# Zero blocks, cell scatters and gather waits rearranged in a graph attention and GCN kernel

## What is computed

```python
q, k, v = (typed_linear(x, W, ntype) for W in (Wq, Wk, Wv))
a  = (typed_rel(k[src], rel_att, etype) * q[dst]).sum(-1) * rel_pri / sqrt(D)
ex = exp(a - segment_max(a, dst)[dst])
h  = segment_sum(typed_rel(v[src], rel_msg, etype) * ex / segment_sum(ex, dst)[dst], dst)
x  = layernorm(x + layernorm(x + gate * typed_linear(h, Wa, ntype) + (1 - gate) * x))
for W, b, g, be in layers:          # three GCN layers, edge weights ew, self loops added
    norm = dinv[src] * ew * dinv[dst]
    h = batch_norm(segment_sum((h @ W)[src] * norm, dst) + b)   # relu between layers
out = layernorm(x + h)
```

## Time and profile before

| what | us |
|---|---|
| median of 3 runs (4591.87 to 4594.39) | 4593.5 |
| the profiled execution | 4592.2 |
| its span | 4590.3 |
| batches 2 to 51, by SP's issues | 1599.9 |
| last attention gather to L537 | 119.9 |
| L537's end to the first dense matmul | 373.2 |

### The profile page before, as it was taken

How to read it: one execution, slowest core, us unless ns; L and a number is a source line. 1 busy time by engine, 2 the same in 40 slices (tenths; PEclk the granted TensorE clock), 3 DMA queues, 4 the chain that set the end, 5 groups by cost and what they waited for, 6 DMA issues and landing times. The chain is left out here.

```text
span 4590.3 us, 52237 instructions
## 1 busy us (share of the span) xinstructions
PE 2969.0 (65%) x14449; PEld 2143.5 (47%) x14449; DVE 2312.5 (50%) x8186; ACT 1147.0 (25%) x2512; POOL 2411.3 (53%) x2514
## 2 busy tenths in 40 slices
PE   3895666666676666664420666777767776767774
PEld 3774656666666656663200433344433444433342
DVE  3774655655655555553522345533455534455435
ACT  1223556555655555552001200000000000000001
POOL 0002544444466666665577266665466664666662
PEclk9998778777787877776755889988899988999987
DMA  4896555565422322221000455555545545555552
GB/s 110 273 358 232 199 200 210 189 216 191 163 88 80 87 79 81 84 81 48 1 1 0 172 190 174 189 191 184 186 174 190 189 174 179 192 188 176 189 189 61
DMA packets 232026, 706.47 MB, mean 154 GB/s; under 512 B 62326, under 2 KB 111957, under 8 KB 212928
## 3 DMA queue, kind: packets, MB, share of 16 engines
q1 hardware_dynamic: 104252, 447.79, 26.7%
q0 software_dynamic: 93184, 191.21, 14.4%
q10 hardware_dynamic: 34308, 64.13, 4.3%
HBM read 559.66 MB, written 143.28 MB: 153 GB/s over the span
## 5 line engine op out<-in xcount | busy, mean ns | idle before, releaser
L552 POOL DMA_INDIRECT stage<-h_tab,earr x1248 | 1183.3, 948 | 810.8 <-issue 346.5
L527 POOL DMA_INDIRECT arena<-kv_tab,idxr x832 | 796.0, 957 | 970.3 <-ACT idxr L634 405.6
L1013 PE MATMUL bank<-arena,xr 128*128 128x512 f32 (+1 forms) x2058 | 1021.1, 638 | 5.6 <-issue 5.6
L992 PE MATMUL bank<-oh,stage 128*128 128x128 f32 x2496 | 394.3, 308 | 494.0 <-issue 487.8
L992 PEld LDWEIGHTS bank<-oh,stage 128*128 128x128 f32 x2496 | 354.1, 214 | 712.3 <-issue 701.1
L860 PE MATMUL bank<-xr,arena 128*128 x3328 | 494.0, 308 | 236.8 <-DVE arena L1254 146.9
L1572 DVE TENSOR_TENSOR sums<-sums,bank 128x128 f32 x1248 | 351.3, 282 | 568.3 <-remote 398.2
L1013 PEld LDWEIGHTS bank<-arena,xr 128*128 128x128 f32 x2058 | 407.6, 212 | 394.8 <-issue 394.8
L860 PEld LDWEIGHTS bank<-xr,arena 128*128 128x128 f32 x3328 | 456.0, 218 | 259.3 <-issue 258.2
L499 POOL DMA_INDIRECT a_tab<-tot,cell x416 | 416.0, 1000 | 261.2 <-DMA arena<-kv_tab,idxr 151.1
L709 ACT ACTIVATE rs<-mv,epsc 128x49 f32<-128x49 f32 (+1 forms) x6 | 1.9, 316 | 2003.3 <-DVE mv L1611 1692.6
(11 more groups left out here) (224 smaller groups left out, 2739.4 us busy)
## 6 DMA issues: line engine op xcount, KB each, us to landing
arena<-a_tab SPq DMA_DIRECT2D x147, 1792.0 KB
a_tab<-stage SPq DMA_DIRECT2D x49, 1792.0 KB
kv_tab<-stage SPq DMA_DIRECT2D x48, 768.0 KB, 8.5
arena<-key_d ACTq DMA_DIRECT2D x52, 512.0 KB, 7.1
arena<-ew_d ACTq DMA_DIRECT2D x52, 512.0 KB, 10.1
arena<-rel_d SPq DMA_DIRECT2D x52, 512.0 KB
stage<-h_tab,earr POOLq DMA_INDIRECT x1248
arena<-kv_tab,idxr POOLq DMA_INDIRECT x832
```

Of the source, the lines that this page charges most:

```text
L527: G.indirect_dma_start(kv[b % 3][:, t, :], None, kv_tab, bass.IndirectOffsetOnAxis(idxr[:, b % 3, t:t + 1], 0))\
L552: G.indirect_dma_start(gring[:, (q % NG) * GRP + s, :], None, h_tab[l], bass.IndirectOffsetOnAxis(src_i[:, t:t + 1], 0)).then_inc(row_land ...
L992: last = M.matmul(bank[q % NG][:, s * P:(s + 1) * P], gring[:, (q % NG) * GRP + s, :], oh[:, q % NG, s, :], start=True, stop=True)
L1013: mm = M.matmul(o_[:, 0:cw], xr[:, n, :], abuf[B % NBUF][:, n % KB, 0:cw], start=n == 0, stop=n == NT - 1)
```

## The change

Three things are done.

1. `zeros_by(b)` becomes `b * NBLK // ZB` with ZB = 46: one zero block for each of batches 1 to 46, two for b = 16, 31 and 46.
2. No scatter stands between gathers. SY = 120 scatters follow the last gather, 296 follow L537.
3. Ahead of every group but the first (batch edges included), POOL waits for three of the four gathers of the group before (`kv_land` at 48) and, through the new semaphores `kv_last`, for the fourth gather of the group before that. DVE and ACT wait for both, so for all four of the group that they use.

```diff
-SB = 28
-SPB = 6
-SY = 48
-ZPB = 2
+SY = 120
+ZB = 46
...
-    zeros_by = lambda b: min(NBLK, ZPB * b)
+    zeros_by = lambda b: min(NBLK, b * NBLK // ZB)
...
+        kv_last = [sem(f"kv_last{a}") for a in range(2)]
...
                 for g in range(NG):
-                    if g:
-                        pool.wait_ge(kv_land[b % 3][g - 1], 64 * (b // 3 + 1))
-                    for t in slots.get((b, g), ()):
-                        scatter(t)
+                    n = NG * b + g
+                    if n:
+                        b_, g_ = (n - 1) // NG, (n - 1) % NG
+                        pool.wait_ge(kv_land[b_ % 3][g_], 48 * (b_ // 3 + 1))
+                    if n >= 2:
+                        pool.wait_ge(kv_last[n % 2], 16 * (n // 2))
                     if b >= 3:
                         pool.wait_ge(vw_ready, NG * (b - 3) + g + 1)
...
-                         .then_inc(kv_land[b % 3][g], 16)
+                         .then_inc(kv_land[b % 3][g] if s < GRP - 1 else kv_last[n % 2], 16)
             for b in range(NB):
                 gather(b)
-            for t in range(first_of, first_of + SY):
+            pool.wait_ge(tot_ready, 1)
+            for j in range(ND):
+                pool.wait_ge(a_zeroed[j], 16 * BPC)
+            for t in range(SY):
                 scatter(t)
...
-            for t in range(first_of + SY, T1):
+            for t in range(SY, T1):
                 scatter(t)
...
-                dve.wait_ge(kv_land[b % 3][g], 64 * (b // 3 + 1))
+                dve.wait_ge(kv_land[b % 3][g], 48 * (b // 3 + 1))
+                dve.wait_ge(kv_last[g % 2], 16 * ((NG * b + g) // 2 + 1))
```

More of the change, by code:

```diff
@@ L98, in gnn @@
     assert NT % KB == 0 and 2 * T1 == ET and T1 <= 512 and 512 * (ND - 1) < WD and WA + TPB <= 512 * ND and GT % GRP == 0
-    assert HALF + WD <= NW and T1 % KT == 0 and zeros_by(SB - 3) == NBLK
+    assert HALF + WD <= NW and T1 % KT == 0 and ZB < NB
     def groups_before(d):
@@ L502, in _ @@
             pool.wait_ge(tabs_complete, 1)
-            slots, first_of = {}, 0
-            for b in range(SB, NB):
-                for k in range(SPB):
-                    slots.setdefault((b, k % NG), []).append(first_of)
-                    first_of += 1
             def gather(b):
@@ L512, in gather @@
                 pool.sem_inc(gathers_begun, 1)
-                if b == SB:
-                    pool.wait_ge(tot_ready, 1)
-                    for j in range(ND):
-                        pool.wait_ge(a_zeroed[j], 16 * BPC)
                 for g in range(NG):
-                    if g:
-                        pool.wait_ge(kv_land[b % 3][g - 1], 64 * (b // 3 + 1))
-                    for t in slots.get((b, g), ()):
-                        scatter(t)
+                    n = NG * b + g
[4 more added lines that the diff above has]
+                        pool.wait_ge(kv_last[n % 2], 16 * (n // 2))
                     if b >= 3:
@@ L632, in indices @@
                     for g in range(NG):
-                        act.wait_ge(kv_land[b % 3][g], 64 * (b // 3))
+                        act.wait_ge(kv_land[b % 3][g], 48 * (b // 3))
+                    for a in range(2):
+                        act.wait_ge(kv_last[a], 16 * (NG // 2) * (b - 2))
                 S.activation(idxr[:, b % 3, :], idx_c[:, bass.ds(b * TPB, TPB)], ACT.Copy).then_inc(idx_ready, 1)
```

## The result

The changed kernel takes 4644.1 us (median of 4 runs, 4632.4 to 4653.8) where the kernel before takes 4592.7 in the same measurement: a ratio of 1.0114, 95% interval 1.010 to 1.0129. It is slower by 1.1%; the forecast was 4557, faster. Its profiled execution takes 4632.4 us with a span of 4630.6, at the lower end of the four, 40.3 us above the span of before. In the changed code the gathers are L518, the scatters L498, the large add is L531 (before: L537), the negative and zero loads of SP are L431 and L438, the first GCN gather L546, the dense matmul L1009, the first matrix load L454.

A forecast was written before the change was run, and what follows sets the result against it. No engine is busy above 65%; POOL's waits for gathers bound free attention batches, scatter bursts slow the stretch behind. Terms -188 + 85 + 68 = -35 against 4592.2 gave 4557 us, range 4445 to 4650.

The forecast's parts named there:

- attention to the last gather: Attention batches: shorter by 188 us, from scatters out about -155, pauses about -130, zeros about +100.
- 72 more scatters ahead of the add: Last gather to L537: the longer burst adds 85 us, bounds +34 and +106.
- 72 more behind it: L537 to the first dense matmul: the longer burst adds 68 us, bounds +55 and +97.
- GCN layers after that: GCN layers behind the first dense matmul: untouched, each keeping its length.
- the free batch, 24.6 us: Attention batch without zeros or scatters: falls from 27.3 to 24.6 us by waiting for the third gather.
- The zero block, 4.7 us,: Attention: a single zero block adds 4.7 us to its batch, as much as a pair does.
- Rival (b): Attention: a single zero block costs half of a pair, 106 us less, total 4451 us; chance 0.11.
- the rule that the prediction cites: DMA queues: an engine alternates between queues with work, packet by packet, so a gather's delay follows from its own packets.
- the factor of 5.7 of the second burst: Scatters behind L537: a pair of tiles slows from 2.45 to 14.05 us; also applied ahead of L537.
- (a): Both scatter bursts: other work proceeds at less than a tenth, +106 and +118, total 4628 us; chance 0.20.
- The 1.47 us a scatter: Scatters behind L537: they complete every 1.47 us, slower than issued, which sets when the matrix loads start.
- (c): Attention: the third gather's landing gives nothing, free batches stay at 27.3 us, total 4689 us; chance 0.09 with its halves.

The follow-up runs named there:

- second chip: Another chip, where both kernels ran again unchanged: before 4340.7 us, the change 4322.7 us, ratio 0.9959.
- the looser waits: POOL waits for all four gathers of the group before last, not three of the last; on the kernel before 3926.5 us, on the change 3985.8 us.
- the change with pairs: The changed kernel with its zero blocks again in pairs, in batches 1 to 25: 4265.4 us, 0.9816 of the kernel before.
- the paced burst: The changed kernel with each scatter waiting until the one four before it has completed: 4319.1 us, 0.9938 of the kernel before.
- the pauses alone: The kernel before with only the change's new POOL waits, zero pairs and scatters left as they were: 4179.1 us, 0.9622.

## Why the prediction was wrong

In the terms of its sum, with the first measurement's profile and the experiments:

| term | forecast | measured first | second chip |
|---|---|---|---|
| attention to the last gather | -188 | -144 | -188 |
| 72 more scatters ahead of the add | +85 | +102 | +93 |
| 72 more behind it | +68 | +76 and +15 in the first layer | +93 |
| GCN layers after that | 0 | -8 | -2 |
| sum | -35 | +40 | -5 |

- **The first step that failed is the free batch, 24.6 us.** Of its four groups, two or three are as worked out: pauses of 1.3 to 1.5 us, periods of 6.0 to 6.5 us in the changed kernel against 7.28. The others, in which or behind which SP's loads are issued, take 6.6 to 8.4 us, and a free batch takes 26.4. On the second chip, where SP issues the loads from 1869.68 to 1871.5, that pause reads 3.31 us beside two of 1.32:

```profile
1864.02 0.95 POOL L518 DMA_INDIRECT arena<-kv_tab,idxr  x1 [1.32 <-DMA arena<-kv_tab,idxr]
...
1870.38 0.95 POOL L518 DMA_INDIRECT arena<-kv_tab,idxr  x1 [1.32 <-DMA arena<-kv_tab,idxr]
...
1878.39 0.95 POOL L518 DMA_INDIRECT arena<-kv_tab,idxr  x1 [3.31 <-DMA arena<-kv_tab,idxr]
```

  DVE's own chain, which I took as 24.0 us, is nearer 23.5: the 6.6 us of waiting fell in a window of 48 us and not in two whole batches, and with the looser waits batches take 23.4 (and 3 x 7.28 + 4 x 1.25 is 26.8, not 26.9). Over batches 7 to 46 the rate missed by 30.27 - 29.3 = 1.0 us, 39 us in all, over the last four by 1.8, 7 us. Two of SP's three loads there are small, 64 KB each, but the third (L426) moves 512 KB. In the 25 free batches of the change with pairs, the first of POOL's pauses that ends more than 3 us behind its issue is 2.9 us on average, the others 1.4. That this load is what holds up the landing is only argued: no run moved it.
- **The zero block, 4.7 us,** was right in kind (one costs what two cost, 3.8 to 4.2) and 0.8 too high, which takes back part of the first error. Rival (b) is refuted. Spreading the blocks cost some 60 us (the change against the change with pairs, on two chips), where I had "about +100" within the sum. The packets around the change's block of 1104.75 show what holds the group up. The group's four gathers are issued from 1104.11 to 1107.86 on the software queue (q0), the block goes on the hardware queue (q1). The DMA rows (packets, MB, share of the engines) of 1107 to 1111 us, and then of 1111 to 1115:

```profile
q1 hardware_dynamic: 395, 1.42, 100.0%
q0 software_dynamic: 3, 0.01, 1.3%
```

```profile
q1 hardware_dynamic: 200, 0.67, 47.0%
q0 software_dynamic: 144, 0.39, 26.4%
```

  For 4 us the block has the engines to itself and the gathers' own packets stand still; they don't take turns with it packet by packet, as in the rule that the prediction cites. With the pair of 1173.73 in the kernel before, none of the gathers' packets moves from 1176 to 1179 us, and then 143 move beside 447 of the block's queue until 1184: the second block runs beside them, which is why two cost hardly more than one.
- **The scatters ahead of the add, +85.** I took 19 us of the burst as work done under it, by the factor of 5.7 of the second burst. The rows show less: DVE's stalls grow with the burst, up to 42.82 us, and the add comes 221.8 us behind the last gather where (a) forecast 226; in the forecast's terms 106 - 102 = 4 us of the work were done under the burst and not 19. The failing step is the use of one burst's factor for the other. On the other chips the size is right for another reason: DVE isn't slowed, is done before POOL, and the 72 issues count in full.
- **Behind the add, +68.** The matrix load follows the add's end by 427 us (forecast 435) and the dense matmul by 449 (441): mis-sized by 8. But I called the GCN gathers harmless, and they start 15 us behind the dense matmul, where before they started 6 us ahead of it; the first layer takes 14.7 us more. That the late gathers are the reason isn't tested by itself, but the kernel with eight scatters a batch shows the same pair: gathers 20 us behind the dense matmul, a first layer 18 us longer. Together +91, close to the upper bound of +97. The 1.47 us a scatter behind it are refuted as a rate by the paced burst; what looked like a rate is a fixed 40 us on the last ones.
- **The chances.** The result is near rival (a) in its first half and between the forecast and (a) in the second; in the free batches it lies two thirds of the way from the forecast to (c) (26.4 between 24.6 and 27.3). That (a)'s sum of +36 meets the measured +40 is luck: its terms were -188, +106 and +118, where -144, +102, +91 and -8 were measured. (a) had 0.20; the forecast's sum of -35 stood on three terms of 68 to 188 us, which turned out to be off by 44, 17 and 23, so more of the chance belonged on the other side.
- **What the forecast didn't look at** is that the waits themselves make zeros and scatters expensive. "POOL idles until the fourth gather has landed" was read as the price of a free batch. It is also what turns one block into 4 us and six scatters into 6 to 8. With the looser waits one or two blocks cost nothing, and six scatters 28.2 - 23.4 = 4.8 us, where POOL's own issuing (27.7) has become the bound; that is no less than the 4.2 beside the new pauses, so the scatters' price didn't go away. Part 1 of the change touches the blocks, part 2 the scatters, and only the third, the waits, works on the cause, and on the kernel before it does better alone (0.9622) than with the other two (0.9959).

Adding up, on the chips of the experiments: pauses -164 us (before to the pauses alone), scatters moved behind the last gather +86, single blocks for pairs +57, together -21, beside the measured -18 to -21. The three are steps of one path from before to the change, so that their sum must agree is no test; what it gives is the price of each part in this order. The second of them by its parts: 144 scatters cost 144 x 1.28 = 184 us behind the gathers and, six a batch beside the new pauses, 24 x 4.2 = 101 among them, which makes +83.

The Trainium skill (DMA: Bandwidth & Descriptors, "Queues, rings and completion order") says that a DMA's semaphore increment lands only after every earlier write of that DMA engine, on whatever queue. For the block above, SP's blocks between 1000 and 1200 us land so long after their issue:

```profile
DMA to landing us min/median/max: 7.5/8.5/10.0
```

The one issued at 1104.75 is the slowest of them and lands 10.0 us later, at 1114.7, and POOL is released at 1115.32: by that rule gathers issued behind a block count as landed only once it is written, which agrees with these times. But the packets above show that the gathers' own data come late too, so the rule isn't needed to explain the pause, and no run here shows what it adds. Looser waits help in either case, since POOL then has the next group under way.

## What to carry to other kernels

Where an issuing engine waits for the transfers just begun, everything else on the queues is paid for in full by that wait; before moving or spreading the other traffic, let the issuer run one group further ahead and price it again (here 9.7% from one wait: the cost of one or two blocks gone, that of six scatters down from 8.3 to 4.8 us a batch, and four blocks still 5.2). An issue costs its time on its engine wherever it stands unless it fills a pause there, so count how many fit under each pause, and leave the rest where another chain is the bound. A forecast that is a small difference of large terms needs the terms from rows of the same stretch, and the sign of a 1% change measured once may not hold on the next chip.

## What was not expected of the hardware

- One transfer of 1792 KB beside the gathers makes a batch 3.8 us longer, two 4.2, four 8.5. While the first drains, the gathers' packets all but stop (3 beside 395 in 4 us).
- The same program takes 4593 us in the first measurement and 4341 to 4350 us in five later ones on five chips. In the first, waits of single DVE instructions for the one before often grow to 1.05 us under a stream of scatters of 128 single words; in the later ones they don't.
- SP goes on 37 to 42 us behind the issue of the last scatter, also when no more than four are under way, and in the first measurement though the DMA engines move nothing for 34 us of it.
- With the looser waits the DMA engines moved 278 GB/s beside 205 in the same stretch: they had not been the limit.
